# Node degrees of a graph layer: summed as four stretches in four column groups, then spread over the partitions

## The reference

```python
h   = relu(layernorm(x))
xn  = batchnorm(h, norm1_g, norm1_b)
agg = segment_sum(xn[src], dst)
deg = segment_sum(ones(E), dst)
agg = agg / maximum(deg, 1.0)[:, None]
conv_out = relu(agg @ W_conv + b_conv)
attn = linear_attention(h)            # one batch entry of 256 columns; all other nodes take its last one
x   = x + batchnorm(conv_out + attn + h, norm2_g, norm2_b)
h   = relu(layernorm(x))              # the second layer sums over the edges, with no division,
x   = x + second_layer(h)             # and then runs two wide matrix products with batch norms
```

## Time and profile before

| | before |
|---|---|
| runs, us | 365.54, 366.03, 366.22 |
| profiled execution, us | 365.55 |
| its span, us | 363.7 |
| TensorE busy | 348.0 us (96%) |
| VectorE busy | 246.4 us (68%) |
| ScalarE busy | 181.3 us (50%) |
| GpSimd busy | 95.2 us (26%) |
| mean granted TensorE clock | 0.998 |

### The profile page before, as it was taken

The page is one execution under the profiler, slowest core; times in us unless marked ns, Lnnn a source line. Parts: engine busy times, 40 slices in busy tenths (PEclk is TensorE's granted clock), DMA queues, the critical chain, the costliest instruction groups (busy, mean ns, idle before and its releaser), DMA issues.

```text
span 363.7 us, 6194 instructions
## 1 busy us (share of the span) xinstructions
PE 348.0 (96%) x2072; PEld 224.0 (62%) x2072; DVE 246.4 (68%) x667; ACT 181.3 (50%) x302; POOL 95.2 (26%) x163
## 2 busy tenths in 40 slices
PE   7899899989999999999998999999999999999994
PEld 3678655757777666767564675455555555565562
DVE  5889999998998995867998787522464443422325
ACT  0548538768477167454437766411534645233132
POOL 8132120000000000100042778722277465101100
PEclk9999999999999999999999999999999999999999
DMA  6990303300000000034900000000000000010223
GB/s 162 289 303 30 119 1 119 118 3 1 3 3 4 3 3 3 3 97 148 264 9 3 0 2 3 2 2 1 2 0 0 2 0 2 0 51 21 70 58 85
DMA packets 13539, 18.05 MB, mean 50 GB/s; under 512 B 1839, under 2 KB 6895, under 8 KB 13491
## 3 DMA queue, kind: packets, MB, share of 16 engines
q1 hardware_dynamic: 12538, 17.21, 16.4%
q10 hardware_dynamic: 953, 0.23, 0.3%
HBM read 14.88 MB, written 2.56 MB: 48 GB/s over the span
## 4 chain that ended last, share of the span: by engine, by line
PE 74%; DVE 15%; issue 4%; ACT 3%; DVEq 2%; DMA 0%; POOL 0%; SPq 0%; ACTq 0%; POOLq 0%
PE bank L1424 71%; DVE ring L988 2%; DVE st L1095 2%; DVE st_row L938 2%; PE bank L1815 1%; PE bank L1454 1%; PE bank L1774 1%; ACT hn L688 1%; DVEq L1137 1%; DVE st_row L1310 1%; DVE x L1305 1%; DVE mv_row L939 1%; DVE x L1375 0%; PE bank L1635 0%; DVE ln_tmp L933 0%
## 5 line engine op out<-in xcount | busy, mean ns | idle before, releaser
L1424 PE MATMUL bank<-AT,hh 125*128 125x400 f16 (+3 forms) x250 | 81.2, 332 | 1.2 <-DVEq L1335 0.4
L1424 PE MATMUL bank<-AT,hl 125*128 125x400 f16 (+3 forms) x250 | 80.9, 332 | 0.0
L988 DVE TENSOR_SCALAR ring<-iota_code,code 125x250 f16<-125x250 f16 x200 | 46.1, 307 | 1.4 <-issue 1.4
L1424 PEld LDWEIGHTS bank<-AT,hh 125*128 125x128 f16 x250 | 24.1, 97 | 19.8 <-issue 1.1
L1424 PEld LDWEIGHTS bank<-AT,hl 125*128 125x128 f16 x250 | 24.2, 97 | 17.6 <-issue 0.2
L1424 PE MATMUL bank<-ring,S 125*128 125x250 f16 x200 | 33.5, 310 | 0.0
L1424 PE MATMUL bank<-a_hi,w_hi 128*128 128x400 f16 (+1 forms) x96 | 32.6, 340 | 0.0
L1424 PE MATMUL bank<-agg_hi,w_hi 128*128 128x400 f16 (+1 forms) x96 | 32.6, 339 | 0.0
L1424 PE MATMUL bank<-agg_hi,w_lo 128*128 128x400 f16 (+1 forms) x96 | 32.5, 339 | 0.0
L1424 PE MATMUL bank<-a_hi,w_lo 128*128 128x400 f16 (+1 forms) x96 | 32.5, 339 | 0.0
L1424 PE MATMUL bank<-agg_lo,w_hi 128*128 128x400 f16 (+1 forms) x96 | 32.5, 339 | 0.0
(11 more groups left out here) (229 smaller groups left out, 703.0 us busy)
## 6 DMA issues: line engine op xcount, KB each, us to landing
w_s<-w SPq DMA_DIRECT2D x4, 1024.0 KB, 5.2
x_in<-x SPq DMA_DIRECT2D x5, 448.0 KB
x<-x SPq DMA_DIRECT2D x2, 1120.0 KB
out<-x SPq DMA_DIRECT2D x6, 224.0 KB
wB<-wk SPq DMA_DIRECT2D x1, 1024.0 KB, 9.6
wA<-wq SPq DMA_DIRECT2D x1, 1024.0 KB, 13.8
wC<-w_conv SPq DMA_DIRECT2D x1, 1024.0 KB, 16.1
wB<-wv SPq DMA_DIRECT2D x1, 1024.0 KB, 6.3
```

The costliest lines, as they stand in the source:

```text
L988: return dve.tensor_scalar(ring[:, slot, j, a:b], iota_code[0:CH, a:b], code[:, bass.ds(c + j, 1)], float(-CODES * t), ALU.subtract, ALU.i ...
L1424: return pe.matmul(o, l, r, start=start, stop=stop, skip_group_check=True)
```

## The change

A `D` group no longer sums all columns of its block over the full width of the array. The block is cut in four stretches of 113 or 100 columns (`quarters`), and each stretch is multiplied with only 32 columns of ones and written to its own 32 partitions of the bank, that is, in its own group of 32 columns of the array. VectorE takes maximum, scale and reciprocal on this short tile, `rdq`. A new group `Ec` then spreads the result: four fp32 matmuls, whose stationary operand is one column of the identity broadcast to 128 columns, write the four stretches into all partitions of another bank, and ScalarE copies it to `rdb`.

`D0` and `D1` move one slot ahead and `E0` and `E1` take their places. In `LAST` the degree group goes ahead of `A31`, and `E2` stands behind `F2`. `D2` is read on VectorE as before; `E2` is copied on ScalarE, between `weight_mean(1)` and `weight_high(1, 0)`. The users of `rdb` now wait for a semaphore of ScalarE, `s_rdb`. Some banks change.

```diff
 SLOTS = [s.split() for s in (
...
-    "MX2 G8", "QT2 G9", "KV2 UK3 D0", "O2 UQ3 A00", "A10", "MX3 A20", "QT3 A30 F1", "KV3 D1 A01",
+    "MX2 G8", "QT2 G9 D0", "KV2 UK3 E0", "O2 UQ3 A00", "A10", "MX3 A20", "QT3 A30 F1 D1", "KV3 E1 A01",
     "O3 A11", "TA0 TA1 A21 WO0 WO1")]
...
+def quarters(c):
+    c0, w = COLS[c]
+    q = -(-w // 4)
+    return [min(g * q, w - q) for g in range(4)], q
...
-LAST = "A31 F2 D2 A02 A12 A22 A32 A33".split()
+LAST = "D2 A31 F2 E2 A02 A12 A22 A32 A33".split()
...
-LAST_BANKS = (6, 4, 0, 1, 2, 3, 7, 5)
+LAST_BANKS = (0, 6, 4, 5, 1, 2, 3, 7, 0)
...
# ScalarE, counts_out
-                if name[0] == "D":
-                    free_group(copy(rdb[:, c0:c0 + w], ps[:, 0:w]), name)
+                if name[0] == "E":
+                    act.activation(rdb[:, c0:c0 + w], ps[:, 0:w], ACT.Copy).then_inc(sem("s_rdb"), 1)
+                    act.wait_ge(sem("s_rdb"), c + 1)
+                    act.sem_inc(free[PLACE[name][0]], 1)
...
             weight_mean(1)
+            counts_out("E2")
             for half in range(2):
                 weight_high(1, half)
...
# VectorE, the pieces D and E
                 elif name[0] == "D":
-                    c0, w = COLS[int(name[1])]
+                    c = int(name[1])
+                    d = rdq[:, 0:quarters(c)[1]]
                     dve.wait_ge(sem("s_bn1"), 1)
-                    d = rdb[:, c0:c0 + w]
-                    if name in LAST:
-                        ps = read_group(dve, name)[:, 0:w]
-                    else:
-                        dve.wait_ge(free[PLACE[name][0]], PLACE[name][1] + 1)
-                        ps = d
+                    ps = read_group(dve, name)[:, 0:quarters(c)[1]]
+                    if c:
+                        dve.wait_ge(full[PLACE[f"E{c - 1}"][0]], PLACE[f"E{c - 1}"][1] + 1)
                     own.step(dve.tensor_scalar(d, ps, 1.0, wscale[:, 0:1], ALU.max, ALU.mult))
-                    n_deg[0] = own.mark(dve.reciprocal(d, d))
-                    if name in LAST:
-                        dve.sem_inc(free[PLACE[name][0]], 1)
+                    dve.reciprocal(d, d).then_inc(sem("s_rdq"), 1)
+                    dve.sem_inc(free[PLACE[name][0]], 1)
+                elif name[0] == "E":
+                    pass
...
# VectorE, mean_rows
-                own.after(n_deg[0])
+                dve.wait_ge(sem("s_rdb"), ci + 1 if ci < NC else NC)
...
# TensorE
                     ps = open_group(pe, name)
-                    ins = accumulate([(ps[:, 0:w], [(ones16[0:L, :], AT[:, k, c0:c0 + w]) for k in range(T)],
-                                       [(ones16[0:L, :], ATlo[:, k, c0:c0 + w]) for k in range(T)])])[0]
+                    starts, w = quarters(int(name[1]))
+                    places = [ps[g * 32:(g + 1) * 32, 0:w] for g in range(4)]
+                    blocks = [slice(c0 + s, c0 + s + w) for s in starts]
+                    ins = sum_up([[(o, ones16[0:L, 0:32], AT[:, k, b]) for o, b in zip(places, blocks)] for k in range(T)],
+                                 [(o, ones16[0:L, 0:32], ATlo[:, k, b]) for k in range(T) for o, b in zip(places, blocks)])
+                elif name[0] == "E":
+                    c = int(name[1])
+                    starts, w = quarters(c)
+                    pe.wait_ge(sem("s_rdq"), c + 1)
+                    ps = open_group(pe, name)
+                    for g, s in enumerate(starts):
+                        ins = mm(ps[:, s:s + w], ident[:, 32 * g:32 * g + 1].broadcast_to([P, P]), rdq[:, 0:w], True, True)
```

More of the change, by code:

```diff
@@ L322, in gnn_kernel @@
         rdb = place("rdb", [P, N], F32, 146)
+        rdq = place("rdq", [P, -(-COLS[0][1] // 4)], F32, 152)
         x1 = place("x1", [L, T, D], F32, 154)
@@ L765, in _ @@
                         conv_high(int(name[1]))
-                    elif name[0] in "AD":
+                    elif name[0] in "AE":
                         counts_out(name)
+                    elif name[0] == "D":
+                        pass
                     else:
@@ L1056, in attention @@
                     dve.sem_inc(free[PLACE[name][0]], 1)
-            n_deg = [0]
             def weight_low(layer, half):
@@ L1682, in accumulate, with sum_up @@
                 return last
+            def sum_up(steps, extra):
+                for o, l, r in steps[0]:
+                    mm(o, l, r, True, False)
+                with pe.If_lt(big_r, most_r):
+                    for o, l, r in extra:
+                        mm(o, l, r, False, False)
+                pe.end_ifs()
+                for n, step in enumerate(steps[1:]):
+                    for o, l, r in step:
+                        ins = mm(o, l, r, False, n == len(steps) - 2)
+                return ins
             seen = pe.alloc_register("seen")
```

## The result

| | before | changed |
|---|---|---|
| median, us | 366.02 (7 runs) | 375.99 (7 runs) |
| lowest to highest, us | 365.54 to 366.22 | 371.51 to 377.51 |
| profiled execution, us | 365.55 | 371.51 |
| its span, us | 363.7 | 369.7 |
| mean granted TensorE clock, profiled | 0.998 | 0.998 |

The changed kernel is slower, by a ratio of 1.0244 (95% interval 1.0216 to 1.0272, with the two longest executions left out). The forecast was 369.5 us, range 368.0 to 371.3. The direction was right, the size was not.

What follows compares the result with a forecast made beforehand. The prediction took TensorE's order, with its waits for VectorE, to bound the kernel. E0 -0.29, E1 +0.76 and E2 +3.03 gave +3.50 us: 369.05 against the profiled 365.55, median 369.5 us, range 368.0 to 371.3.

Steps and rivals of the forecast that it cites:

- E2: Spreading group behind F2 in `LAST`, forecast very late and deciding: A02 starts at 179.03 instead of 176.00, 3.03 us lost.
- Its stand-still: At E2, TensorE stands 3.06 us, since VectorE does seven statistics of 3.64 us before D2's step.
- the release of `rdq`: Before E2, VectorE begins D2's step of 1.08 us at 176.94 us, so `rdq` is ready at 178.02.
- E1's late start: At E1, TensorE waits 0.8 us for `rdq`, ready at 148.29; A01 starts at 149.30, 0.76 us lost.
- The reciprocal of 100 columns: In VectorE's step between D and E: 6.25 ns per element, so 0.78 us for 100 columns.
- D0: First short D group on TensorE: four column groups overlap, 0.62 us plus 0.10 per group, 0.72 against 1.91.
- E0: First spreading group on TensorE: four fp32 matmuls, eight records, 0.90 us, with `rdq` ready on time.
- E0's block: At D0 and E0, the window follows at 119.16 us instead of 119.45: 0.29 us gained.
- my price by it: At D0, by the tiling-mode drain rule alone, D0 and D1 would lose 0.4 us more each; not adopted.
- the row: Earlier trace at 31.35 us: eight records of 256 columns in four column groups took 0.57 us, so they overlap.
- the clock falls in the gap: Rival at E2's stand-still: TensorE's clock drops to 1.2 GHz, costing 1.3 us, so 370.8 us; chance 0.24.
- two bounds in the earlier trace: For the clock rival: full clock in a 1.60 us gap, 0.52 from 362.00 on, after the last matmul at 359.74.

## Why the prediction was right in part and wrong in size

**What held.** The chain is TensorE's, and the place that decides is E2. Its stand-still was forecast at 3.06 us and measured at 3.02; the release of `rdq` at 178.02, measured 178.9 with everything 0.8 us later. E1's late start was forecast to push A01 by 0.76 - 0.29 us, measured 0.80. The reciprocal of 100 columns, 0.78 us by the line through two rows, measured 0.78.

**D and E, the exchange.** D0 was put at 0.72 us. Its stream is at the pace of four matmuls abreast, but 0.79 us pass to the window's first matmul, and 0.09 us stand ahead of D0, behind G9's last matmul (113.55 less 113.24 and the 0.22 from start to start). E0 was put at 0.90 and takes 0.98. So E0's block gained 0.04 us, not 0.29; in the sum this is a quarter of a microsecond. With the 0.09 us ahead of it D0 cost 0.88 us. Of that, 0.40 us lie outside a stream of 0.48, where my 0.72 allowed 0.24. The Trainium skill says that a change of tiling mode drains the array ("TensorEngine Tiling (Array Packing)", Key Properties); my price by it, 0.4 us more than the row, would have been 1.12. The measured 0.88 lies between the two, somewhat nearer to the row. No run separates a drain from other costs at the two ends of the group.

**What failed first: the clock.** The step was "the clock falls in the gap", with 0.24 of the chance and 1.3 us as its price. Of the 13 executions of the changed kernel 12 have a mean clock of 0.995 or less and take 372.65 us or more; the one with 0.998 took 371.51. In one of the 12 the profile shows the fall at E2, and in the profile of the one at 0.998 there is none. The fall at E2 alone costs about 2.5 us at the median, by filled against not filled, where I had 1.3. My price came from the slow matmuls at the start of the execution. That was a poor source: the profile's clock column reads 1.00 there, so these rows don't show what a fall costs. Behind E2 the clock stayed down for 3.40 us in one profile, which cost 1.66 us, and for 6.80 us in another, which cost 2.8. Both errors point the same way. I had two bounds in the earlier trace rows, no fall in 1.6 us and a low clock 2.3 us after the last matmul, and 3.06 lies beyond both, so it should have been the likeliest case.

**What failed second: a term that wasn't there.** I counted how many instructions TensorE executes, never how long its program is. 30 more matmuls in each of three D groups and 30 more in each of three branches shift everything behind them. At the branch near 230 us the shift costs 2.0 us in the profiled execution (2.42 less the 0.43 of the kernel before), and probably a second fall of the clock in others. Shown: a shift alone removes the stop from the changed kernel and makes it in the kernel before. Not shown: a second fall in the changed kernel itself, whose two profiles have stops of 2.42 and 2.28 us with the clock at 1.00. It is seen behind stops of 2.02 and 2.35 us in two of the variants.

Together: 366.0 + 3.9 for the waits + 2.0 for the stop is 371.9, near the one execution with a full clock, 371.5. The distance to 376.0, 4.5 us, goes with the mean clock: (0.998 - 0.986) of 374 us is 4.5 us, lost at TensorE's pace. This is an estimate, since the mean also counts the time after the last matmul, in which the clock is low and costs nothing. How it divides between the two places in a single execution stays open, as only two executions of the changed kernel left a profile, and none of the slower ones.

## What to carry to other kernels

When a result makes a detour over another engine, look up what stands in that engine's own list ahead of the step, not how long the step takes: a step of 1.1 us cost 3.0 us because 3.6 us of other work came first, and moving it in the list, not making it faster, was the cure. A stand-still of 3 us on TensorE between dense matmuls cost nearly its own length again in clock, in most executions though not in all; fill it or shorten it. In a long unrolled program with branches over code that never runs, measure a change at two or three program lengths before believing 0.5% either way.

## What the runs showed of the hardware

Where code lies can cost more than what it does: 152 instructions that never execute made the kernel before 2.8 us slower at the median (368.79 against 365.95), in the profile through one stop of 2.35 us and the clock's fall behind it. In the profiles that have the stop it takes 1.39 to 2.42 us; in those with a better position of the code it is gone. The granted clock fell at a stand-still of 3.02 us in one profile and stayed up at the same one in another; after 1.46 and 1.6 us it was at 1.00. Four column groups of 32 run fully abreast: of the 0.69 us of D0's forty matmuls 0.21 is the latency of one, which leaves 0.05 us for each of the ten steps of 113 columns. And a broadcast fp32 column costs 0.98 us for 450 columns, where two fp16 passes over the same columns take 0.42.
